# Written-out attention and expert loops, inverse roots spread by DMA, and a normalised row's remainder made on POOL

## The reference

```
for i in range(4):
    h = _ln(x, cms_ln_g[i], cms_ln_b[i])
    h = gelu(h @ cms_W1[i] + cms_b1[i])
    x = x + h @ cms_W2[i] + cms_b2[i]
```

## Time and profile before

| what | value |
|---|---|
| median of 3 runs | 505.76 us |
| profiled execution | 510.27 us, of which the span from the first to the last instruction is 508.5 us |
| busy in the span | PE 439.5 us (86%), DVE 381.7 (75%), ACT 323.7 (64%), POOL 156.3 (31%) |
| chain of waits | PE 71%, DVE 12%, ACT 9%, issue 5%, POOL 2% |
| granted clock, whole span | 0.876 |

### The profile page before, as it was taken

One profiled execution on the slowest core, in us unless ns is written; L12 is line 12 of the kernel. 1 busy time (PEld: TensorE's weight loads), 2 busy tenths in 40 slices (PEclk: granted clock), 3 DMA queues, 4 the chain that ended last, 5 costly groups with the idle time before them and its releaser, 6 DMA issues.

```text
span 508.5 us, 7061 instructions
## 1 busy us (share of the span) xinstructions
PE 439.5 (86%) x2081; PEld 361.9 (71%) x2081; DVE 381.7 (75%) x931; ACT 323.7 (64%) x530; POOL 156.3 (31%) x368
## 2 busy tenths in 40 slices
PE   3857579999999999999999959686868499999996
PEld 2754368888888888888889948575756367878774
DVE  4965665888888888888875974877775778989894
ACT  1135375888888888888894143443337388989893
POOL 0236543233333333333301772637273200000000
PEclk9986797999999999999997566665668589999999
DMA  6500000000000000000000000000000000000000
GB/s 240 218 1 0 1 1 1 1 1 1 0 1 0 2 1 2 0 1 0 1 0 2 1 1 1 1 0 1 0 0 1 1 1 11 10 10 10 10 12 21
DMA packets 7477, 7.22 MB, mean 14 GB/s; under 512 B 5140, under 2 KB 5912, under 8 KB 7192
## 3 DMA queue, kind: packets, MB, share of 16 engines
q1 hardware_dynamic: 7448, 6.87, 4.1%
HBM read 5.82 MB, written 1.05 MB: 14 GB/s over the span
## 4 chain that ended last, share of the span: by engine, by line
PE 71%; DVE 12%; ACT 9%; issue 5%; POOL 2%; DMA 0%; DVEq 0%; SPq 0%; ACTq 0%; POOLq 0%
PE ps L1246 60%; PE ps L1267 3%; PE ps L1275 3%; ACT w_all L712 2%; PE ps L1403 2%; PE ps L1440 1%; ACT hid L706 1%; PE ps L1553 1%; DVE stats L797 1%; DVE x L821 1%; DVE st L1028 1%; DVE st L934 1%; DVE qmax L977 1%; ACT x L595 1%; DVE hid L1216 1%
## 5 line engine op out<-in xcount | busy, mean ns | idle before, releaser
L867 DVE TENSOR_TENSOR hid_lo<-hid,hid_hi 128x1024 fp32r<-128x1024 f32 x64 | 78.4, 1225 | 46.6 <-ACT hid_hi L562 46.6
L557 ACT ACTIVATE hid<-ps,b_fold 128x512 f32<-128x512 f32 x128 | 83.8, 682 | 37.2 <-PE ps L1246 37.2
L1246 PE MATMUL ps<-xn_hi,w_all 128*128 128x512 f32 x256 | 90.2, 414 | 0.0
L1246 PE MATMUL ps<-hid_hi,w_all 128*128 128x512 f32 x256 | 84.2, 390 | 0.0
L562 ACT ACTIVATE hid_hi<-hid 128x1024 fp32r<-128x1024 f32 x64 | 67.8, 1060 | 2.0
L1246 PEld LDWEIGHTS ps<-xn_hi,w_all 128*128 128x128 f32 x256 | 50.0, 195 | 10.0
L1246 PEld LDWEIGHTS ps<-hid_hi,w_all 128*128 128x128 f32 x256 | 48.2, 188 | 10.4 <-DVE hid_lo L867 0.4
L1246 PE MATMUL ps<-xn_lo,w_all 128*128 128x512 f32 x128 | 51.3, 401 | 0.0
L706 ACT ACTIVATE hid<-ps,eb_fold 128x512 f32<-128x512 f32 x64 | 43.9, 689 | 10.2 <-PE ps L1246 10.2
L1246 PE MATMUL ps<-hid_lo,w_all 128*128 128x512 f32 x128 | 49.8, 389 | 0.0
L1216 DVE TENSOR_TENSOR hid<-hid,ps 128x512 f32<-128x512 f32 x64 | 43.6, 682 | 6.4 <-ACT hid L706 6.3
(11 more groups left out here) (221 smaller groups left out, 905.1 us busy)
## 6 DMA issues: line engine op xcount, KB each, us to landing
hh<-in_tokens SPq DMA_DIRECT2D x8, 256.0 KB, 8.0
hid<-in_w SPq DMA_DIRECT2D x2, 1024.0 KB, 8.9
out<-hh SPq DMA_DIRECT2D x8, 128.0 KB, 2.0
ew_raw<-in_expert_w SPq DMA_DIRECT2D x1, 512.0 KB, 10.1
ew_raw<-in_expert_w SPq DMA_DIRECT2D x1, 256.0 KB, 10.3
cons<-in_constants SPq DMA_DIRECT2D x1, 233.0 KB, 2.6
wqkv_raw<-in_w_qkv SPq DMA_DIRECT2D x1, 192.0 KB, 10.6
rows<-in_rows SPq DMA_DIRECT2D x1, 100.5 KB, 3.0
```

Source lines behind the costliest of these rows:

```text
L557: act.activation(hid[:, j % 2, f, :], bank[f], ACT.Gelu, bias=b1_fold[:, j // B * F + f:j // B * F + f + 1]).then_inc(gelu_done, 1)
L867: dve.tensor_tensor(hid_lo[:, j % 2, 2 * p:2 * p + 2, :], hid[:, j % 2, 2 * p:2 * p + 2, :], hid_hi[:, j % 2, 2 * p:2 * p + 2, :].bitcast( ...
L1246: return pe.matmul(out, lhsT, rhs, start=start, stop=stop)
```

## The change

- **Inverse roots by DMA.** PE's `broadcast` is kept for rows j = 0 to 2 of the 32. For j = 3 to 31 SP stores the 128x4 roots of the row in HBM and loads them back spread over all partitions (`rstd_row`); DVE's `norm_x` reads that tile from SBUF, with a step of four values. Statistics are taken one turn earlier (row j+3 in turn j).
- **The remainder of a normalised row** (`x_lo`) is made by DVE for j = 0 and 1 and by POOL for j = 2 to 31, each one behind the inverse root of the row two further on.
- **Attention**: all loops are written out; `g_out` is multiplied into a second copy of the output weights, so PE makes a plain and a gained output (128 columns instead of 64) and ACT copies 512 columns instead of 256. DVE's centring and scaling become four instructions per row on 128x64 with scalars per partition, where they were two on 128x256; the scaled output with its base becomes four, where it was three on 128x256. Some waits of the last turn are placed otherwise. PE waits for the gained weights ahead of the head.
- **Experts**: all loops are written out; the remainder of the hidden tile is made by POOL for 6 of 8 experts and by DVE for experts 0 and 4; `copy_sum` comes after iteration 11, 19, 27 ... for every row. Stores are issued by SP in a plain loop.
- The `alone` increments are gone.

```diff
+XLO_BY_DVE = 2
+SPREAD_BY_PE = 3
+LO_BY_DVE = (0, 4)
...
@@ SP
+            for j in range(SPREAD_BY_PE, L * B):
+                slot = j % 4
+                sp.wait_ge(rstd_ready, B + j + 1)
+                sp.dma_start(roots_hbm[slot].rearrange("(p t) -> p t", t=NT), rstd[:, slot, :]).then_inc(rstd_stored, 16)
+                sp.wait_ge(rstd_stored, (j - SPREAD_BY_PE + 1) * 16)
+                sp.wait_ge(normed, B + j - 3 + FREE)
+                sp.dma_start(rstd_row[:, slot, :], roots_hbm[slot].partition_broadcast(P)).then_inc(rstd_loaded, 16)
...
@@ POOL, layers
-                alone(pool, "pool")
...
-            for n in range(B, B * (L + 1)):
-                inverse_root_of_row(n, n % 4)
+            def x_lo(j):
+                pool.wait_ge(xhi_ready, j + 1)
+                pool.tensor_tensor(xn_lo[:, j % 2, :], xn[:, j % 2, :], xn_hi[:, j % 2, :].bitcast(fp32),
+                                   ALU.subtract).then_inc(xlo_by_pool, 1)
+
+            for n in range(B, B * (L + 1) + 2):
+                if n < B * (L + 1):
+                    inverse_root_of_row(n, n % 4)
+                if n - B - 2 >= XLO_BY_DVE:
+                    x_lo(n - B - 2)
...
@@ POOL, experts
+            for n in range(UNITS):
+                if n % E in LO_BY_POOL:
+                    hidden_lo(n)
...
@@ ACT
-                act.activation(at(h1, b), bank[4 * k + 1][:, 2 * P:4 * P], ACT.Copy).then_inc(o_ready, 1)
+                act.activation(o_sb[:, k, :, :].rearrange("p w n -> p (w n)"), bank[4 * k + 1],
+                               ACT.Copy).then_inc(o_ready, 1)
...
+            for n in range(AHEAD, UNITS + 4):
+                if n < UNITS:
+                    gelu(n)
+                if n <= UNITS:
+                    hidden_hi(n - 1)
+                if n % E == SKEW and n >= E:
+                    copy_sum(n // E - 1)
...
@@ DVE, layers
             def norm_x(j):
-                dve.wait_ge(rstd_bc, j + (B + 1))
-                dve.tensor_tensor(xn[:, j % 2, :], x[:, j % B, :], bank[BB], ALU.mult).then_inc(normed, 1)
+                if j < SPREAD_BY_PE:
+                    dve.wait_ge(rstd_bc, j + (B + 1))
+                    dve.tensor_tensor(xn[:, j % 2, :], x[:, j % B, :], bank[BB], ALU.mult).then_inc(normed, 1)
+                else:
+                    dve.wait_ge(rstd_loaded, (j - SPREAD_BY_PE + 1) * 16)
+                    by_tile = rstd_row[:, j % 4, :].rearrange("p (q t) -> p t q", t=NT)
+                    dve.tensor_tensor(tiles(xn[:, j % 2, :], P), tiles(x[:, j % B, :], P), by_tile,
+                                      ALU.mult).then_inc(normed, 1)
...
-                if j + 2 < L * B:
-                    row_stats((j + 2) % 4, j + (B + 3))
+                if j + 3 < L * B:
+                    row_stats((j + 3) % 4, j + (B + 4))
...
-                if 0 < j < L * B - 1:
+                if 0 < j and j + 1 < XLO_BY_DVE:
                     x_lo(j + 1)
...
@@ DVE, attention
             def scaled_output(b, k):
                 dve.wait_ge(r2_ready, b + 1)
-                own.inc(dve.tensor_tensor(tiles(t_sb[:, k, :]), tiles(at(h1, b)), per_tile(r2[:, k, :], D2), ALU.mult))
...
+                dve.wait_ge(res_ready, b + 1)
+                for t in range(NT):
+                    tile = slice(t * D2, (t + 1) * D2)
+                    last = dve.scalar_tensor_tensor(h1[:, b, :][:, tile], o_sb[:, k, 1, tile], r2[:, k, t:t + 1],
+                                                    h0[:, b, :][:, tile], ALU.mult, ALU.add)
...
-            both(expert_centred, B - 2)
+            dve.wait_ge(ezlo_ready, B - 2)
+            both(expert_z, B - 2)
             top_two(0)
-            both_own(expert_z, B - 2)
             both(expert_z_lo, B - 2)
...
@@ PE
-                pe.wait_ge(xlo_ready, j + 1)
+                if j < XLO_BY_DVE:
+                    pe.wait_ge(xlo_ready, j + 1)
+                else:
+                    pe.wait_ge(xlo_by_pool, j - XLO_BY_DVE + 1)
...
-                if j + 2 < L * B:
-                    turn(x[:, (j + 2) % B, :], x_ready, j + 3, j + (B + 2))
-                if j + 1 < L * B:
+                if j + 3 < L * B:
+                    turn(x[:, (j + 3) % B, :], x_ready, j + 4, j + (B + 3))
+                if j + 1 < SPREAD_BY_PE:
                     broadcast((j + 1) % 4, j + (B + 1))
...
+            pe.wait_ge(wout_gained, 1)
```

More of the change, by code:

```diff
@@ L71, with units_before @@
 NCON = 466
+LO_BY_DVE = (0, 4)
+LO_BY_POOL = tuple(e for e in range(E) if e not in LO_BY_DVE)
+UNITS = B * E
+def units_before(n, of):
+    return n // E * len(of) + sum(e < n % E for e in of)
 class Own:
     def __init__(self, engine, semaphore):
-        self.engine, self.semaphore, self.base, self.n = engine, semaphore, 0, 0
+        self.engine, self.semaphore, self.n = engine, semaphore, 0
     def inc(self, instruction):
@@ L82, in inc @@
         self.n += 1
-        return self.base + self.n
+        return self.n
     def wait(self, value):
         self.engine.wait_ge(self.semaphore, value)
[L88 to L95, removed]
 def build(nc, tok_in, emb_in, wupd_in, wf_in, w1_in, w2_in, headw_in, cols_in, rows_in, cons_in,
@@ L652, in _ @@
             act_turn(0, True, False)
-            with act.Fori(1, B // 2 - 1) as g:
+            for g in range(1, B // 2 - 1):
                 act_turn(g, True, True)
@@ L1141, in _ @@
             dve_turn(0, True, False)
-            with dve.Fori(1, B // 2 - 1) as g:
-                own.enter(g, TURN_OWN, 1)
+            for g in range(1, B // 2 - 1):
                 dve_turn(g, True, True)
-                own.leave(B // 2 - 2)
             dve_turn(B // 2 - 1, False, True)
@@ L1243, in _, with output @@
+            def output(b):
+                dve.wait_ge(yt_done, b + 1)
+                dve.tensor_tensor(h1[:, b, :], bank[6 + b % 2][:, 0:NT * D2], h1[:, b, :], ALU.add).then_inc(out_ready, 1)
+            for n in range(UNITS + 6):
+                if n < UNITS:
+                    dve_job(n)
+                if 1 <= n <= UNITS and (n - 1) % E in LO_BY_DVE:
+                    hidden_lo(n - 1)
+                if n % E == SKEW + 2 and n >= E:
+                    output(n // E - 1)
         @block.tensor
@@ L1539, in _ @@
                 k_transposes(k, k)
-            with pe.Fori(0, B // 2 - 1) as g:
+            for g in range(B // 2 - 1):
                 pe_turn(g)
@@ L1621, in _ @@
             for b in range(HALF):
                 turn_gates(b)
[L1624 to L1625 removed]
+            for n in range(4):
+                hidden(n)
             pe.wait_ge(gates_copied, HALF)
[L1628 to L1629 removed]
+            spread_gates(0)
+            bias_sum(0)
             pe.wait_ge(gates_ready, 4)
[L1632 to L1634 removed]
+            spread_gates(1)
@@ L1645, in _ @@
-            pe_experts(B // 2 - 1, False)
+            for n in range(AHEAD, UNITS + 5):
+                if n == E:
+                    pe.wait_ge(gates_copied, B)
+                if n < UNITS:
+                    hidden(n)
+                    spread_gates(n)
+                    if n % E == 0:
+                        bias_sum(n)
+                if n - SKEW < UNITS:
+                    second_products(n - SKEW)
+                if n % E == SKEW + 1 and n >= E:
+                    turn_sum(n // E - 1)
```

325 lines of the change are left out of this document (128 added, 197 removed).

## The result

The changed kernel takes 535.86 us (median of 4 runs, 532.11 to 537.17), against 506.2 us (505.65 to 507.66) for the kernel before in the same comparison: 1.057 times as long, 95% interval 1.051 to 1.063. The forecast was 524.6, with a range of 496 to 530. The direction was right, the size was 11 us short, and the time lies above the range. The profiled execution took 537.17 us, its span 535.4, with a granted clock of 0.882.

What follows compares the result with a forecast made beforehand. PE was taken as full in the layers. Terms 20.5 - 1.3 + 0.7 + 1.1 - 2.2 = +18.8 on the profiled 510.27 us gave 529.1, and 524.6 as median; range 496 to 530.

Steps and rivals of the forecast that it cites:

- What bounds the kernel, and the overlaps: Layers: PE fills the 6.33 us turn; DVE instructions with two SBUF inputs and POOL's SBUF reads exclude each other.
- Part 1, roots by DMA: Layers: PE loses four transposes, 0.43 us a turn; the DMA, landing after 4 to 10 us, is taken as hidden.
- the doubled `norm_x`: Layers, rival: the step doubles norm_x, turn 7.75 us, time 541; all cases above 529 together got 0.12.
- Part 2, x_lo on POOL: Layers: x_lo waits behind POOL's root and DVE is held; 7.12 us a turn, 0.79 more, +20.5 over 26 turns.
- rival "POOL keeps up": Layers: DVE and POOL hardly hold each other, turn 6.09 us, time 497.9; chance 0.24 for 491 to 500.
- the cheap one that I had: Layers: when the power gets in first, turns of 6.40 and 7.15 us alternate, mean 6.78, time 515.8.
- rival "the clock": Layers: PE, idle 1.2 us a turn, falls to 1.2 GHz, over 90 us more; called small, within 0.12 above 529.
- Turn 1, "0 (1 either way)": Layers, turn 1: it waits for POOL before and after the change, so no difference, within 1 us either way.
- Part 3, head: Head: PE waits for the gained weights behind five short DVE instructions, +0.7 us, between 0 and 1.5.
- Part 4, attention: Attention: wider and extra PE passes against shorter DVE work, zero for three turns; at the end +1.1, between -1 and +3.
- Part 5, experts: Experts: earlier copy of the sum gains 4.4 us, POOL's slower remainder costs 1.6 and 0.6; -2.2, between -4.4 and +2.
- the last term of the sum: Whole kernel: the median was taken 4.5 us below the profiled run, as before, turning 529.1 into 524.6.

Runs made afterwards that it cites:

- the version with neither edit: Changed kernel with the layers' roots spread by PE and x_lo by DVE as before, changed attention and experts kept: 496.24 us, 0.981 of the kernel before.

## Why the prediction was right in direction and wrong in size

- **What bounds the kernel, and the overlaps: right.** PE was full, and a transpose taken from it was time gained, 6.35 to 5.98 us a turn with `x_lo` on DVE (5.90 forecast). The holding of DVE and POOL stands in every turn with both.
- **Part 1, roots by DMA: hidden, as forecast** (5.4 us to landing, between 4 and 10), and the wait appears only when the root is moved back or its store is slow. **The step that failed is here: "Its step of four values has no row: between nothing and twice the time; I take nothing".** It was 1.067 us (median) instead of 0.67, more than halfway to the upper bound. The reason given, one value a cycle for both inputs, does not hold with the step: the plain read of the same row takes 0.670. The rule of the Trainium skill that the prediction had as a rival ("SBUF — State Buffer", § Door 1: The DMA port swizzle) says that each access that crosses to a new 16-byte line pays a penalty; a step of four fp32 values does that with every value. The trace agrees for this read: 0.40 us on 512 values. The same note also says that one can stride for free as far as 4 fp32 values; taken as a step of four, this read does not bear it out. No run has another step, so that the line is what makes it long is argued and not shown. I had the doubled `norm_x` in view with its price, 541, and gave the times above 529 a part of 0.12; the bound should have weighed more, since no row spoke for zero.
- **Part 2, x_lo on POOL: the working was right within 0.02 us a turn once the step is taken out.** Forecast 7.12 a turn, measured 7.14; forecast +19.2 for the layers, measured +19.7; L409, the power and `h_lo(.,1)` held as told. That the layers' sum fits to 0.5 is in part luck: from one residual to the next 24 turns and not 26 grew by 0.79 (+19.1), the first two together got 0.7 shorter, and the last five together 1.4 longer, where I had the last three 1.3 shorter. The rival "POOL keeps up" is what happens with the row in PSUM. With the step I had 7.75: measured are 7.42 in the steady half, since only one more instruction is caught (L415), and irregular turns of 7.7 on the mean in the first half, where the first 15 turns cost 7.4 us more than in the run without the step. An alternation is there, but not the cheap one that I had: its long turn at full clock takes 8.4 us, and the four long turns at a lower clock take 0.4 to 1.7 more, some 4 us in all by that one turn (an estimate). That is a small share of the rival "the clock".
- **Turn 1, "0 (1 either way)": two errors that cancel.** With the statistics a turn earlier the layers gain 5.6 us; the wait for POOL's first `x_lo` gives them back.
- **Part 3, head: right.** PE waits 0.84 us for the gained weights, forecast 0.7.
- **Part 4, attention: mis-sized.** Forecast +1.1, with part 3 +1.8; measured -4.1 for both. Of it 2.9 us are `attend`, 12.9 us over the four turns before and 10.0 after, and 1.4 us PE's idle time ahead of the contexts. I had counted the passes at the length that they had in the kernel before, without seeing that the clock was at 0.50 there. In the turn at 353.6 us the clock is 0.53 for 8.6 us and then 1.00; in the corresponding turn of before it is 0.50 for 11.6 us and 0.61 in the next 3.6. What brings it up earlier I did not settle; that it is not the product's width was shown. Part of the -4.1 may be the one profiled execution of the kernel before, which took 4.5 us more than the median: against that execution the version with neither edit gains 7.7 us behind the layers, by the medians (496.24, 505.57) only some 3.
- **Part 5, experts: both terms right in kind, the net too hopeful by 2.6.** The early copy gains 0.8 to 1.0 us a row, where 1.1 was forecast for four rows. POOL's remainder costs 3.5 to 4.8 us of the profiled stretch from the first GELU and 2.2 to 3.2 of the median, where I had 2.2. Together they come to +0.4.
- **The sum.** Without the step the profiled execution was 524.25, against a forecast of 529.1: -2.8 ahead of the layers, +0.5 in them, -5.1 in head and attention, +2.6 in the experts. With the step it was 537.17, 8.1 above. The other 3.2 us of the 11.3 by which the median missed are the last term of the sum: "The median of the runs is 4.5 below the profiled run; the same difference" was 1.3 for the changed kernel. Of the medians the one without the step, 526.29, is 1.7 from the forecast; by the parts above that is closer than the working deserved.

## What to carry to other kernels

When an operand moves from PSUM to SBUF, count it as two changes: its access pattern may cost time (here 1.6 times with a step of four values), and the instruction begins to hold POOL. Look for the loop that the held engine is in: here both were nearly free with slack on POOL, and cost some 39 us without. Where POOL is held, an instruction that PE waits for is badly placed behind a chain of small ones (moving it ahead was worth some 24 us); where nothing held the chain, the same place let PE keep its turn of 6.35. And an unknown term for which no row speaks is better taken at its bounds than at zero.

## What the runs showed of the hardware

- DVE's product of two SBUF tiles of 512 fp32 columns takes 0.67 us plain and 1.07 with one input at a step of four values (16 bytes); with that input in PSUM it took 0.67. With both in SBUF it holds POOL: a POOL instruction of 0.20 us took 0.57 beside the plain one, 0.97 beside the one with the step, and 0.20 beside the one from PSUM.
- POOL's subtraction of 1.26 us stretched a DVE one of 1.22 that began 0.16 behind it to 2.18.
- A store of 2 KB from 128 partitions landed after 1.4 us in 16-byte packets and after 11.2 in 4-byte packets.
- A pass of PE with 128x128 weights takes 0.115 to 0.119 us with 64 columns and 0.128 with 128, at the 2.4 GHz level.
- After idle stretches of 2.6 to 3.9 us PE's clock was granted at the 1.2 GHz level for part of the next turn in most cases: 0.66 from 75 to 85 us around the wait of 2.7 in the kernel before, 0.73 in the changed kernel from 138 to 148 us behind one of 2.62. Behind another of 2.62, at 99.87, it stayed at 1.00. The waits of 1.2 us in each steady turn left it at 1.00.
